# Attention block with routed experts: the products of W1 with beta for two experts in each of four drain slots, and the scaling by gamma two experts at a time in the slots behind

## The reference, cut to what matters

```python
def _sublayer(xs, g, b, W1e, b1e, W2e, b2e):
    mu = jnp.mean(xs, axis=-1, keepdims=True)
    var = jnp.mean(jnp.square(xs - mu), axis=-1, keepdims=True)
    h = (xs - mu) * jax.lax.rsqrt(var + EPS) * g + b
    return xs + jax.nn.relu(h @ W1e.T + b1e) @ W2e.T + b2e
```

## Time and profile before

| | |
|---|---|
| median of three runs | 1318.54 us (1316.46 to 1320.81) |
| the profiled execution | 1319.99 us, its span 1318.1 us |
| mean granted TensorE clock | 0.976 of full speed |
| busy share of the span | TensorE 95%, VectorE 90%, ScalarE 81%, GpSimd 69% |
| TensorE busy tenths, slices 33 to 35 of 40 (1054 to 1153 us) | 9, 4, 9 |

### The profile page before, as it was taken

One profiled execution on the slowest core, in us unless ns is written; L12 is line 12 of the kernel. 1 busy time (PEld: TensorE's weight loads), 2 busy tenths in 40 slices (PEclk: granted clock), 3 DMA queues, 4 the chain that ended last, 5 costly groups with the idle time before them and its releaser, 6 DMA issues.

```text
span 1318.1 us, 40452 instructions
## 1 busy us (share of the span) xinstructions
PE 1246.7 (95%) x12156; PEld 1102.7 (84%) x12156; DVE 1188.0 (90%) x4716; ACT 1064.2 (81%) x3176; POOL 909.7 (69%) x1343
## 2 busy tenths in 40 slices
PE   6999999999999999999999999999999994999992
PEld 5898888888888888888888888888888884788782
DVE  4999999999999999999999999999999984799993
ACT  4998888888888888888888888888888872566661
POOL 3567777777777777777777777777777663388886
PEclk8999999999999999999999999999999996899996
DMA  5000000000000000000000000000000003122210
GB/s 219 6 9 14 13 12 12 12 12 12 12 12 12 12 12 12 12 12 12 12 12 12 12 12 12 12 12 12 12 8 9 11 10 86 45 59 60 62 58 6
DMA packets 38505, 31.89 MB, mean 24 GB/s; under 512 B 4882, under 2 KB 35734, under 8 KB 38080
## 3 DMA queue, kind: packets, MB, share of 16 engines
q1 hardware_dynamic: 31696, 21.47, 5.4%
q0 software_dynamic: 4656, 8.81, 1.9%
q10 hardware_dynamic: 2112, 1.11, 0.3%
HBM read 20.35 MB, written 12.07 MB: 25 GB/s over the span
## 4 chain that ended last, share of the span: by engine, by line
PE 77%; DVE 13%; issue 5%; POOL 2%; ACT 1%; DMA 1%; DVEq 0%; SPq 0%; POOLq 0%; ACTq 0%
PE psZU L647 15%; PE psS L592 14%; PE psZU L662 12%; PE psP L624 10%; PE psZU L650 6%; PE psT L606 5%; PE psT L607 4%; PE psT L608 4%; DVE ff L374 2%; DVE wup_s L391 2%; DVE nscore L869 1%; DVE on L400 1%; POOL out L453 1%; DVE gg L409 1%; PE psM L690 1%
## 5 line engine op out<-in xcount | busy, mean ns | idle before, releaser
L1126 POOL TENSOR_TENSOR prob<-prob,rinv 128x256 f32<-128x256 f32 (+1 forms) x512 | 413.2, 829 | 281.3 <-DVE rinv L887 280.6
L746 ACT ACTIVATE prob<-nscore,nmax 128x128 f32<-128x128 f32 (+1 forms) x1024 | 454.6, 451 | 9.7 <-DVE nmax L869 9.2
L869 DVE CUSTOM_DVE_ANT_0 nscore<-psS,mask 128x128 f32<-128x128 f32 (+1 forms) x1024 | 321.1, 351 | 1.8 <-PE psS L592 1.0
L878 DVE TENSOR_TENSOR p_lo<-psP,p_hi 128x768 fp32r<-128x768 f32 x256 | 243.7, 952 | 3.0 <-ACT p_hi L716 3.0
L716 ACT ACTIVATE t_hi<-psT 128x512 fp32r<-128x512 f32 x256 | 153.0, 598 | 115.1 <-PE psT L608 112.3
L857 DVE TENSOR_TENSOR t_lo<-psT,t_hi 128x512 fp32r<-128x512 f32 x256 | 175.6, 686 | 53.9 <-ACT t_hi L716 50.5
L716 ACT ACTIVATE p_hi<-psP 128x768 fp32r<-128x768 f32 x256 | 206.8, 808 | 3.5 <-PE psP L624 3.5
L746 ACT ACTIVATION_READ_ACCUMULATOR prob<-nscore,nmax 128x1 f32 x1024 | 199.4, 195 | 0.0
L892 DVE TENSOR_TENSOR z_lo<-psZU,z_hi 128x512 fp32r<-128x512 f32 x256 | 175.4, 685 | 5.5 <-ACT z_hi L716 2.3
L592 PE MATMUL psS<-t_hi,t_lo 64*128 64x128 f32 (+1 forms) x1024 | 164.6, 317 | 1.4 <-DVE nmax L869 1.4
L606 PE MATMUL psT<-xt_hi,qk_lo 128*128 128x256 f32 x512 | 157.6, 308 | 3.6 <-DVE t_lo L857 2.2
(11 more groups left out here) (171 smaller groups left out, 3297.4 us busy)
## 6 DMA issues: line engine op xcount, KB each, us to landing
fin<-routed_rows SPq DMA_DIRECT2D x40, 136.0 KB
wx<-ffn_w SPq DMA_DIRECT2D x2, 2058.0 KB, 12.2
xin<-x SPq DMA_DIRECT2D x32, 128.0 KB, 2.2
xres<-x SPq DMA_DIRECT2D x32, 128.0 KB, 2.1
out<-res,fin POOLq DMA_INDIRECT x80
routed_rows<-padr ACTq DMA_DIRECT2D x4, 272.0 KB, 4.8
routed_rows<-padr SPq DMA_DIRECT2D x4, 272.0 KB, 4.4
wup_s<-wup SPq DMA_DIRECT2D x1, 1024.0 KB, 4.9
```

The source lines that it names most:

```text
L746: last = nc.scalar.activation(prob[:, pb, h, a:z], nscore[:, (s - lag) % 2, h, a:z], ACT.Exp, bias=nmax[:, pb, h, q:q + 1], scale=-1.0, ac ...
L869: last = v.tensor_tensor_reduce(nscore[:, n1, h, a:z], psS[:, h, a:z], mask[:, a:z], -1.0, -MASKED, ALU.add, ALU.min, nmax[:, p1, h, q:q + 1])
L878: v.tensor_tensor(by_half(p_lo, s % 2), psPh, by_half(p_hi, s % 2).bitcast(F32), ALU.subtract).then_inc(S["p_split"], 1)
L1126: last = g.tensor_tensor(pr, pr, rinv[:, p2, :, q:q + 1].broadcast_to([P, 2, z - a]), ALU.mult)
```

## The change

The eight products with beta are made two experts at a time in the drain slots 1 to 4, and none in slot 7. The scaling of W1 by gamma, eight instructions in slot 7 of ScalarE's program before, is spread over its slots 2 to 5, two in each; the slot waits for the products of its two experts, made a slot earlier. Behind them the final waits count four: `weights_ready` has four steps in place of one, and the sum with b1 in slot 9 of VectorE waits for `bias_done` at 4 in place of 5. The number of matmuls, scalings and DMAs stays as it was.

```diff
@@ ffn_act
-            act.wait_ge(S["weights_ready"], 1)
+            act.wait_ge(S["weights_ready"], E // 2)
@@ tensor, slot
                 if not live(0) and 1 <= s <= E // 2:
-                    first_bias(range(s - 1, s))
-                if not live(0) and s == 7:
-                    first_bias(range(E // 2, E))
+                    first_bias(range(2 * s - 2, 2 * s))
@@ scalar, slot
-                if not live(0) and s == 7:
-
-                    act.wait_ge(S["bias_done"], E // 2 + 1)
-                    for e in range(E):
+                if not live(0) and 2 <= s <= E // 2 + 1:
+
+                    act.wait_ge(S["bias_done"], s - 1)
+                    for e in range(2 * s - 4, 2 * s - 2):
                         last = nc.scalar.activation(wx[:, e, 0:FB * P], wx[:, e, 0:FB * P], ACT.Copy,
                                                     scale=gam[:, e:e + 1])
                     last.then_inc(S["weights_ready"], 1)
@@ vector, misc_early
                 if not live(0) and s == 9:
 
-                    dve.wait_ge(S["bias_done"], E // 2 + 1)
+                    dve.wait_ge(S["bias_done"], E // 2)
```

## The result

Eighteen executions of the changed kernel took 1320.32 to 1330.21 us, median 1326.02; eighteen of the kernel before 1316.05 to 1321.13, median 1317.74. The medians lie 8.3 us apart, the means 7.7. The ratio is 1.0058 (95% interval 1.0044 to 1.0072): slower by 0.6%, which is 7.6 us. Two executions far outside are left out of every comparison: one of the kernel before at 1509 us and one of the kernel with only scalings moved at 2330 us. The forecast was 1320.6 and no difference that can be told; the range ended at 1324.8. The outcome is the rival called A, to which 0.10 was given.

The account below looks back on a forecast made before the run. The prediction took the chain ending last to lie on TensorE for 77% of the span, running without a gap in drain slots 1 to 4. Terms 3.15 - 0.8 - 0.3 + 0 = +2.05 us gave 1320.6 us, range 1317.8 to 1324.8.

Parts of the forecast that it names:

- rival A: Drain slots: clock falls to 1.2 GHz, TensorE's pieces double, 4.0 us per slot so spent; 6.1 in all, 1324.6 us; chance 0.10.
- The sum: Whole kernel: 3.15 - 0.8 - 0.3 + 0 = +2.05 us, forecast 1320.6 us against the median of 1318.54.
- The clock, row and rule: Passage on TensorE's granted clock: 1.00 over slots 1 to 4, 0.51 from 1096.4 to 1102.8 despite busy L582.
- Part 1: Drain slots 1 to 4: four more matmuls each on TensorE's path, 4 x 0.79 = +3.15 us.
- Part 2: ScalarE's slots 2 to 5: two scalings each, covered by the added L582, 0 us (bounds 0 and 1.5).
- Parts 3 and 4: Slot 7: without L582 `st3` starts 0.8 us earlier; without the scaling on ScalarE `ft` starts 0.3 us earlier.
- The pads: Pad DMAs of ScalarE and SP: start 3.15 us later, land by 1110.6, before block 31's scatter at 1114.5.
- signs listed as wrong: Profile after: clock below 1.00 before block 31's attention-output transposes, TensorE idle in slots 2 to 4, or scatter awaiting pads.
- Rivals B, C and D: B: 11.4 us gained, 1310.3, chance 0.03; C: drain has room, 1319.0, 0.09; D: ScalarE bounds slots, 1322.1, 0.08.
- The 11.4 us of the chain of before: Slot 7: 6.36 us of L582, then 5.01 us of ScalarE scaling, which the chain read alone says could be had.

## Why the prediction was wrong

**The step that failed** is the clock. The sum has no term for it, and the prediction put it aside in "The clock, row and rule" and in rival A. The mechanism was named there, in the right place. Wrong was its chance, 0.10, and the reason given for it: "61% of each slot stays work that held the clock so far, with no idle time". That sentence took the smaller share of wide work for a safe one, and no row showed that it was. The two groups of the executions put thirteen of eighteen on the other side, and of the four profiled executions of the change the one long one has the fall, in slots 2 and 3, and the three others have none up to the end of slot 4.

**The price of rival A** came out near by some luck. "TensorE's pieces double" is too much: L624, L647, L650 and L662 grew by a factor of 1.6 to 1.8 and L582 by 1.9, and a slot at the low clock cost 3.4 us, not 4.0. On the other side a fall outlasted the one slot that was priced: about 10 us in the caught execution, for 4.6 us, and over 15 in that of the run with slot 7 filled, for 7.8. The long executions, 1325.7 to 1330.2 us, all lie above the 1324.6 of the rival.

**Was there a hint?** The three executions before lay 4.35 us apart, and the prediction read this as the measurement's noise. The kernel before has slower executions at a lower mean clock of its own: beside the first experiments eight of 25 took 1318.4 to 1321.8 us at 0.973 to 0.976. But the trace at hand does not put their time in the drain. The profiled execution before, 1319.99 us at 0.976, is one of that kind, and its clock is 1.00 over slots 1 to 4. Beside it stands the profile of the kernel with only scalings moved, 1316.64 us, whose clock is 1.00 there too. Their spans differ by 3.3 us, and 1.7 of it lies behind the table, where the clock comes back later in the expert stage. The windows of the first and then of the second:

```profile
1122.00:1130.00 8.00, 6.59 (x17) 4.86 (x17) 2.10 (x8) 3.17 (x7) 0.00 (x0) 0.50 0.36 87
```

```profile
1122.00:1130.00 8.00, 6.60 (x28) 5.24 (x27) 4.20 (x16) 3.57 (x9) 0.00 (x0) 0.87 0.22 58
```

So part of the spread lies outside the drain: behind the table the profiled executions of all the kernels here took 199.3 to 201.9 us. Whether any execution of the kernel before has a fall in the drain stays open.

**Part 1** (+3.15) was right in kind and a little small. L582 x16 takes 1.68, not 2 x 0.79, so a slot grew by 0.89: 3.6 us in all. No room was found in the slots.

**Part 2** (0) was right: `p_lo` came 1.1 us before its use, the scaling-only run cost nothing, and the products alone cost all.

**Parts 3 and 4** (-0.8, -0.3) were right. `st3` waits for `pay`, and `ft` began 0.02 after its transposes (1109.01 + 0.70 to 1109.73). **The pads** never held the scatter. Together: 3.6 - 1.1 = 2.5, against 2.44 in the profile. One of the signs listed as wrong is there even in the short execution: the clock was at 0.50 when the transposes of block 31's attention output ran (L705, 0.66 us from 1099.20, in place of 0.41). They are not in the chain of waits there.

**Rivals B, C and D** did not happen. The 11.4 us of the chain of before were not there to be had: the change took both pieces out and gained 1.1.

**The sum:** +7.6 us (0.58% of 1317.7; 8.3 by the medians) is made of 2.4 in every execution, and some 5 on the whole that go with the lower clock. The two long executions with a profile, 4.6 and 7.8 us in the drain, are of the size to give them; the other long ones had no profile.

## What to carry to other kernels

Matmuls with a single column keep TensorE busy in the profile and did no more for its clock here than idle time. When they are added to a stretch on the critical path, price the stretch at both clocks, and look at the times of many executions and not at one profile alone. The profile of one execution showed nothing wrong here; a mean clock per execution that goes with its time did. Where in the kernel that lower clock lies, only a profile of a slower execution tells. Put such work where TensorE has nothing else to do, as in the kernel with the products in slots 7 and 14.

## What the runs showed of the hardware that had not been expected

The same program on the same data ran its drain at a granted clock of 1.00 in one execution and at 0.50 for about 10 us in another (0.51 over 15 us in the longest seen, of a kernel whose drain slots 1 to 4 are the same), with the same instructions before it and TensorE busy throughout. The page "TensorE: Matmul & The Clock Gate" of the Trainium skill, section "What's actually happening", says that the point at which the clock changes differs from run to run of one kernel; the traces agree, and show that in this drain it was open not only when the clock falls but whether it does: 1320.19 us without a fall and 1325.79 with one. The same section puts the time lost while the clock comes up, for modelling, at less than 1% of a typical kernel. A fall in the middle of a kernel is another case; the one caught here took 4.6 of 1325.8 us, 0.35%, which is of that size too, and yet it was twice the change's own effect of 2.4 us.
